# Heads of the last batch loaded early, row table and tile levels early, and 52 unread products in TensorE's waits, in an attention and mixture-of-experts block on one core

## The reference

```
x = x + attention(layernorm(x))                 # heads -> ctx @ W_O
xf = layernorm(x).reshape(-1, D)
logits = xf @ Wr / temp
topw, topi = top_k(logits, 2); topw = softmax(topw)
for e in range(8):
    a, g = split(xf @ W1[e] + b1[e])
    y = a * silu(g) @ W2[e] + b2[e]
    out += y * (weight of e for the token, 0 if not chosen)
x = x + out
```

## Time and profile before

| | before |
|---|---|
| median of 3 runs | 1049.57 us (1048.76 to 1050.04) |
| profiled execution | 1049.65 us, span 1047.8 us |
| busy PE, DVE, ACT, POOL | 958.1, 782.6, 555.0, 508.1 us |
| clock granted to TensorE, mean | 0.94 of full speed |
| chain that ended last: PE, DVE, DMA, ACT | 78%, 8%, 5%, 3% |

### The profile page before, as it was taken

How to read it: one execution, slowest core, us unless ns; L and a number is a source line. 1 busy time by engine, 2 the same in 40 slices (tenths; PEclk the granted TensorE clock), 3 DMA queues, 4 the chain that set the end, 5 groups by cost and what they waited for, 6 DMA issues and landing times.

```text
span 1047.8 us, 21901 instructions
## 1 busy us (share of the span) xinstructions
PE 958.1 (91%) x5804; PEld 574.1 (55%) x5805; DVE 782.6 (75%) x2291; ACT 555.0 (53%) x1202; POOL 508.1 (48%) x972
## 2 busy tenths in 40 slices
PE   4999899999999999999989956299999999999993
PEld 2444243333333333333345546288888888888883
DVE  3675999999999999999966556466766666676762
ACT  1555067777777777777763535143433334434431
POOL 5555536666666666666633745543322323233232
PEclk9999589999999999999997966599999999999998
DMA  3688966485867867644456588753555375333332
GB/s 98 215 266 213 234 137 153 93 257 99 257 153 216 250 156 209 150 90 89 89 149 184 188 217 275 224 161 52 140 134 131 50 210 136 55 50 56 54 51 35
DMA packets 107729, 156.53 MB, mean 149 GB/s; under 512 B 26944, under 2 KB 82240, under 8 KB 105088
## 3 DMA queue, kind: packets, MB, share of 16 engines
q1 hardware_dynamic: 83696, 128.03, 45.8%
q0 software_dynamic: 13296, 17.77, 9.8%
q10 hardware_dynamic: 10656, 9.78, 3.5%
HBM read 90.46 MB, written 64.69 MB: 148 GB/s over the span
## 4 chain that ended last, share of the span: by engine, by line
PE 78%; DVE 8%; DMA 5%; ACT 3%; issue 2%; POOL 1%; ACTq 1%; SPq 0%; DVEq 0%; POOLq 0%
PE bank L860 13%; PE bank L881 13%; PE bank L842 13%; PE bank L2020 6%; PE bank L2022 6%; PE bank L2021 6%; PE bank L2050 3%; PE bank L2052 3%; PE bank L2051 3%; PE bank L2034 3%; PE bank L1632 2%; DMA e_rows<-slot_rows 2%; DVE a_xn L314 2%; PE a_ckv L363 2%; PE bank L1996 1%
## 5 line engine op out<-in xcount | busy, mean ns | idle before, releaser
L816 ACT ACTIVATE b_prob<-bank 128x512 f32<-128x512 f32 (+3 forms) x768 | 311.9, 507 | 79.7 <-PE bank L860 78.9
L842 PE MATMUL bank<-b_k_st,b_q_st 96*128 96x512 bf16 (+3 forms) x768 | 255.6, 346 | 5.8 <-DVE b_neg_max L770 1.7
L770 DVE CUSTOM_DVE_ANT_0 bank<-bank,b_mask_max 128x256 f32<-128x256 f32 (+3 forms) x512 | 241.6, 510 | 22.2 <-PE bank L842 22.0
L860 PE MATMUL bank<-b_q_st,b_k_st 99*128 99x512 bf16 (+3 forms) x768 | 242.9, 334 | 4.0 <-ACT b_prob L816 2.0
L726 POOL TENSOR_SCALAR_AFFINE_SELECT b_prob<-b_prob 128x128 f32<-128x128 f32 x512 | 147.0, 300 | 188.5 <-ACT b_prob L816 184.2
L1846 POOL DMA_INDIRECT out_dram<-e_y,e_token x71 | 110.5, 1557 | 238.6 <-issue 158.0
L773 DVE TENSOR_REDUCE b_neg_max<-bank 128x1 f32<-128x512 f32 x256 | 175.8, 687 | 13.4 <-PE bank L842 11.2
L881 PE MATMUL bank<-b_prob,b_v_aug 128*32 128x512 f32 (+3 forms) x1536 | 146.3, 500 | 0.0
L842 PEld LDWEIGHTS bank<-b_k_st,b_q_st 96*128 96x128 bf16 x768 | 75.9, 99 | 109.3 <-DVE b_neg_max L770 52.1
L860 PEld LDWEIGHTS bank<-b_q_st,b_k_st 99*128 99x128 bf16 x768 | 74.8, 99 | 106.3 <-ACT b_prob L816 79.1
L2020 PE MATMUL bank<-w_ring,e_rowsT_hi 128*128 x284 | 125.3, 441 | 3.5 <-DVE e_rowsT_lo L1871 2.2
(11 more groups left out here) (203 smaller groups left out, 1470.7 us busy)
## 6 DMA issues: line engine op xcount, KB each, us to landing
w_parts<-w_ring SPq DMA_DIRECT2D x10, 1536.0 KB, 7.3
w_ring<-w_parts SPq DMA_DIRECT2D x10, 1024.0 KB, 7.6
e_rows<-slot_rows ACTq DMA_DIRECT2D x74, 129.0 KB, 2.1
w_raw<-in_L_ffn_W SPq DMA_DIRECT2D x8, 1024.0 KB, 5.2
ctx_cols<-b_ctx_out SPq DMA_DIRECT2D x16, 512.0 KB
q_parts<-a_part_q SPq DMA_DIRECT2D x8, 768.0 KB, 4.0
k_parts<-a_part_k SPq DMA_DIRECT2D x8, 768.0 KB, 4.8
b_q_st<-q_parts SPq DMA_DIRECT2D x16, 384.0 KB, 5.0
```

The source lines that it names most:

```text
L770: nc.vector.tensor_tensor_reduce(scores, scores, mask_max[:, HALF - width:HALF], -1.0, -MASKED, ALU.add, ALU.min, to).then_inc(max_done, 1)
L816: nc.scalar.activation(prob[n % NP][:, 0:width], prob_ps[n % NS][:, 0:width], ACT.Exp, scale=SCALE).then_inc(prob_ok, 1)
L842: nc.tensor.matmul(out[:, 0:width], q_st[g % RING][0:STACK, h, i * P:(i + 1) * P], k_st[g % RING][0:STACK, h, half * HALF:half * HALF + wi ...
L860: nc.tensor.matmul(prob_ps[n % NS][:, 0:width], k_st[g % RING][0:MAXROWS, h, j * P:(j + 1) * P], q_st[g % RING][0:MAXROWS, h, q0:q0 + widt ...
```

## The change

- The heads of batch 3 go to a buffer of their own, `last_heads`, in the last stage of the weight ring (the rows below and the order show it as `w_raw`), whose weights are loaded only in the expert stage. So `load_heads(3)` no longer waits for `project(2)`, and SP issues it right behind `load_den(3)`, ahead of `store_inverse(3)`.
- SP waits for `c_scale` of batch 3 to land before it stores x2 of batch 2 and what follows.
- DVE does `scale_heads(3)` ahead of `slots(1)`.
- DVE works out `m_tile_row` first among the tables; `level_ok` and `tile_row_ok` are signals of their own. ACT reads the first three levels as soon as they are there, starts its loads at `tile_row_ok`, and splits the first tile's rows between its second and third load. PE transposes the first tile's rows before it waits for the tables.
- PE does 12 products of 128x512 ahead of `counts(1)` and 40 behind `counts(3)`, into the bank `wide[-1]`, from weights that lie in `w_ring`.

```diff
+        self.last_heads = weights.raw[:, W_STAGES, 0, 0:DC * SEQ].rearrange("p (c n) -> p c n", c=DC)
...
+        self.jumped = self.fresh[:].bitcast(F32)
...
+    def heads_of(self, b):
+        return self.heads[:] if b < BATCH - 1 else self.last_heads
+
     def load_heads(self, sp, b):
-        if b:
+        if 0 < b < BATCH - 1:
             sp.wait_ge(self.proj_ok, b * PAIRS)
...
         self.load_den(sp, 3)
+        self.load_heads(sp, 3)
         self.store_inverse(sp, 3)
         self.load_scale(sp, 3)
-        self.load_heads(sp, 3)
         self.load_x(sp, 3)
+        sp.wait_ge(self.scale_in_ok, 16 * DC * BATCH)
         self.store_x2(sp, 2)
...
             then(nc.vector.tensor_reduce(tile_f[:], passed[:], AX.X, ALU.add))
+            then(nc.vector.tensor_tensor(passed[:], passed[:],
+                                         self.jump[:].unsqueeze(1).to_broadcast([P, TABLE, SEGMENTS]),
+                                         ALU.mult))
+            then(nc.vector.tensor_reduce(self.jumped, passed[0:1], AX.X, ALU.add))
+            then(nc.vector.tensor_tensor(same[:], self.row_of_tile[:], self.jumped, ALU.add))
+            then(nc.vector.tensor_scalar(self.tile_row[:], same[:], float(EXPERTS * REGION), None, ALU.min))
+            dve.sem_inc(self.tile_row_ok, 1)
...
         choose(1)
+        scale_heads(3)
         slots(1)
         filled_by_two()
-        scale_heads(3)
         shift(2)
...
+    def spare_products(self, pe, batches, count):
+
+        pe.wait_ge(self.x2_ok, batches * PAIRS)
+        for n in range(count):
+            self.nc.tensor.matmul(self.wide[-1][:], self.weights.ring[:, 0, 0, 0:P], self.weights.ring[:, 0, 0, 0:CHUNK],
+                                  start=True, stop=True)
...
+        self.spare_products(pe, 3, 12)
         self.counts(pe, 1)
...
         self.counts(pe, 3)
+        self.spare_products(pe, 4, 40)
...
-        act.wait_ge(route.tables_ok, 1)
+        act.wait_ge(route.level_ok, 1)
+        levels = [level_of(n) for n in range(AHEAD)]
         route.rows_written(act, BATCH - 2)
         route.tokens_written(act)
+        act.wait_ge(route.tile_row_ok, 1)
         for n in range(AHEAD):
-            load(n, n)
-        rows_high(0, 0)
+            load(n, n, levels[n])
+            if n == 1:
+                rows_high(0, 0)
...
+        rows_turned(0, 0)
         pe.wait_ge(route.tables_ok, 1)
-        rows_turned(0, 0)
         steps(pe, step)
```

More of the change, by code:

```diff
@@ L1077, in __init__ @@
         self.tables_ok = sem("r_tables_ok")
+        self.tile_row_ok = sem("r_tile_row_ok")
+        self.level_ok = sem("r_level_ok")
     def follow(self, turn_bank, prob_sc_ok, prob_ok, pv_ok, max_done, rows_ok, v_aug_ok, acc_out, ctx_st):
@@ L1311, in scale_heads @@
         def scale_heads(b):
+            heads = self.heads_of(b)
             dve.wait_ge(self.heads_in_ok, 16 * (b + 1))
@@ L1316, in scale_heads @@
                 half = slice(k // DC * CHUNK, (k // DC + 1) * CHUNK)
-                nc.vector.tensor_tensor(self.heads[:, k % DC, half], self.heads[:, k % DC, half],
+                nc.vector.tensor_tensor(heads[:, k % DC, half], heads[:, k % DC, half],
                                         self.scale[:, k % DC, half], ALU.mult).then_inc(self.heads_ok, 1)
@@ L1462, in full_tiles @@
             nc.vector.scalar_tensor_tensor(out=self.tile_level[:], in0=self.tile_index[0:1, :],
-                                           scalar=self.full_two[0:1, 0:1], in1=level[:], op0=ALU.is_ge, op1=ALU.add)
+                                           scalar=self.full_two[0:1, 0:1], in1=level[:], op0=ALU.is_ge,
+                                           op1=ALU.add).then_inc(self.level_ok, 1)
         def pad_slots():
@@ L1501, in tables @@
             then(nc.vector.tensor_scalar(same[:, 1:TABLE], same[:, 1:TABLE], 1.0, None, ALU.mult))
-            then(nc.vector.tensor_scalar(self.fresh[:], same[:], -16.0, 16.0, ALU.mult, ALU.add))
-            then(nc.vector.tensor_tensor(passed[:], passed[:],
-                                         self.jump[:].unsqueeze(1).to_broadcast([P, TABLE, SEGMENTS]),
-                                         ALU.mult))
-            then(nc.vector.tensor_reduce(tile_f[:], passed[:], AX.X, ALU.add))
-            then(nc.vector.tensor_tensor(same[:], self.row_of_tile[:], tile_f[0:1, :], ALU.add))
-            nc.vector.tensor_scalar(self.tile_row[:], same[:], float(EXPERTS * REGION), None,
-                                    ALU.min).then_inc(self.tables_ok, 1)
+            nc.vector.tensor_scalar(self.fresh[:], same[:], -16.0, 16.0, ALU.mult, ALU.add).then_inc(self.tables_ok, 1)
             dve.wait_ge(self.tables_ok, 1)
@@ L1930, in _, with level_of, load @@
     def _(act):
-        def load(n, c):
+        def level_of(n):
+            return act.value_load(entry(route.tile_level, n), min_val=1, max_val=3)
+        def load(n, c, level=None):
             act.wait_ge(y_ok, n + 1)
-            level = act.value_load(entry(route.tile_level, n), min_val=1, max_val=3)
-            act.wait_ge(landed, level)
+            act.wait_ge(landed, level_of(n) if level is None else level)
             act.sem_inc(load_turn, 1)
```

4 lines of the change are left out of this document (2 added, 2 removed).

## The result

The changed kernel is slower: 1053.51 us (median of 6; 1052.86 to 1055.58) against 1049.43 (median of 6), ratio 1.0045 with a 95% interval of 1.0031 to 1.0058. The forecast was 1044.3.

What follows compares the result with a forecast made beforehand. It took the kernel as bound by the chain up to the first expert product, with a fixed distance behind it. Normalise(3) earlier -1.7, tables -3.6 and products 0 made -5.3 on 1049.65: 1044.3 us, own range 1042 to 1046.5.

Steps and rivals of the forecast that it cites:

- I take 603.0, just behind the heads: SP's queue, batch 3: the inverse store lands and c_scale is issued at 603.0, bounds 601.97 and 603.6.
- I take 11.9 ... L = 614.9.: Batch 3's c_scale load takes 11.9 us and lands at L = 614.9, bounds 612.5 and 616.6.
- L + 18.8: POOL's scatter branch: batch 1's rows land and free first_row[1] for normalise(3) 18.8 us after c_scale lands, at 633.7.
- L + 17.4: Projection branch: project(3) lets normalise(3) start 17.4 us after c_scale lands, at 632.3, earlier than the scatter branch.
- Slower: Rival: the c_scale wait before slots(1) costs more than the tables give, c_scale landing past 620.2; 1052.4 us; chance 0.04.
- 14.6 us: From batch 3's normalisation to its logits on DVE, the work stays the same 14.6 us.
- Row table and levels early: -3.6.: Tables, ACT's first loads and PE's transposes bring the first expert product 3.6 us earlier, bounds -2.7 and -3.9.
- a first expert product later than 670: Sign that the prediction is wrong: the first expert product comes later than 670 in the new trace.
- The 12 products: 0: PE ahead of counts(1): 12 products delay counts(1) to 612.2 without cost or gain, 0.
- The 40 products ... 0: PE behind counts(3): the clock is lost again before the first expert product, so 0, with -2.6 as other end.
- a kept clock: Rival: the products hold the clock and the expert stage starts warm, 2.6 us more gained, 1041.7 us; chance 0.2.
- The end of the kernel lies a fixed distance behind the first expert product.: Expert stage: PE is busy 337.62 of 350 us, so only moving the first expert product's start, or the clock, counts.

Runs made afterwards that it cites:

- b_heads_behind: The changed kernel, with batch 3's heads in their own buffer but issued behind the c_scale loads; 1052.83 us, 1.0031 to the kernel before.
- a_dve_old: The changed kernel, with DVE doing slots(1) ahead of scale_heads(3) again; 1050.95 us, 1.0015 to the kernel before.
- y_after_no_y: The changed kernel, its first three loads of rows skipping y_ok and the first rows' splitting waiting for the last table; 1053.46 us, 1.0035 to before.
- c_no_products: The changed kernel without its 12 and 40 unread products; 1052.8 us, 1.0030 to the kernel before.
- m_46_products: l_all_early with 46 unread products behind the last counts; 1048.01 us, 0.9979 to the kernel before.
- d_tables_only: The kernel before with only the early row table, levels, loads and transposes; 1050.41 us, 1.0006 to the kernel before.
- n_weights_behind: l_all_early with expert 3's weights issued behind the last rows' landing; 1043.22 us, 0.9954 to the kernel before.
- u_split_weights: n_weights_behind with the last third of expert 3's weights issued eight tiles later; 1043.32 us, 0.9948 to the kernel before.
- j_act_early: d_tables_only with ACT's copy of batch 3's rows behind the third load and Silu's table loaded in ACT's idle stretch; 1052.67 us, 1.0027 to before.
- l_all_early: j_act_early with the first three loads of rows not waiting for y_ok; 1047.28 us, 0.9981 to the kernel before.
- o_46_weights_behind: m_46_products with expert 3's weights issued behind the last rows' landing; 1048.72 us, 0.9986 to the kernel before.
- p_before_weights_behind: The kernel before with only expert 3's weights issued behind the last rows' landing; 1053.02 us, 1.0033 to the kernel before.
- q_after_weights_behind: The changed kernel with only expert 3's weights moved behind the last rows' landing; 1056.46 us, 1.0071 to the kernel before.

## Why the prediction was wrong

*"I take 603.0, just behind the heads"*, for the inverses' landing. The order was right; `b_heads_behind`, without the heads ahead, has `c_scale` issued 2.2 us behind the store. The size was not: the heads took 8.2 us and not 6.3, and the inverses landed at 605.1. That is 606.6 in the frame of before, 3.6 later than forecast and outside the bound of 603.6. The prediction said that no row of before shows a small store behind a large load. The trace has one: SP issued batch 1's heads at 544.43, and they took 13.5 us; batch 2's inverses, issued behind them at 547.98, took 10.2 us and landed at 558.2, just behind the heads. I had not looked there.

*"I take 11.9 ... L = 614.9."* With the inverses this is the failing step that costs most. Counted as in the prediction, from the inverses' landing, `c_scale` took 13.0 us and not 11.9: it did not get faster without the heads beside it. In the seven kernels whose scaling waited for it, the scaling began 12.7 to 13.7 us behind its issue. So the scaling came at 618.22, which is 619.7 in before's frame, past the bound of 616.6; of the 4.8 us that L was too early, 3.6 are the inverses' and 1.2 `c_scale`'s. Underneath lies a wrong picture: that the wait was the heads' and would shrink if they came early. The heads early on SP's queue (25.1 to 27.0 us behind the ctx_cols store, in five kernels), late from their own buffer (25.9), early on another queue (25.9 and 25.3) or as before (24.5 to 26.9, in ten kernels) all end in the same place. Between the end of attention and the scaling about two megabytes and a chain of three small transfers share the same engines, and what goes first was paid by what came next.

*"L + 18.8"* and *"L + 17.4"*. Both branches were right in form: the scatter gated the normalisation at L + 19.5, and `a_dve_old` showed the other at L + 17.3. With L too early by 4.8, the rival *Slower* was what happened up to here. It was worked out as a scale load of 17 us; nearly the same lateness came in two pieces, 4.8 us of extra inverse store and 13.0 of load. I gave it 0.04 because I put the price on one transfer and not on the chain. Normalise(3) was to come 1.7 us earlier and came 3.8 later (46.45 against 42.66): 5.5 us of the miss. With DVE's old order, in `a_dve_old`, it came at 43.16: 2.1 us of that difference are the order's, 1.2 come from a scaling that was earlier in that trace.

*"14.6 us"* from the normalisation to the logits held: 14.63.

*"Row table and levels early: -3.6."* From the logits to the first expert product it was 23.90 and became 22.42, so -1.5. The missed part is the wait for `y_ok` in `load`. I had costed what DVE's table and ACT's reads do, and not gone through every wait of the function that issues. `y_after_no_y` gives 20.26, which is -3.6: the sum was right, the gate on it was not seen. That is 2.1 us of the miss. The sign set for this, a first expert product later than 670, came true (674.74).

*"The 12 products: 0"* and *"The 40 products ... 0"* held in the time (`c_no_products`), and the clock was lost at the place named. The Trainium skill (TensorE: Matmul & The Clock Gate, Part 1) wants idle gaps avoided. `m_46_products` left gaps of only 1.04 and 1.36 us ahead of the first expert product, and its clock stayed at 1.00 up to it, in agreement with that. The prediction priced a kept clock at 2.6 us; the median shows no gain, and the trace says why: the faster PE came sooner to rows that weren't there.

*"The end of the kernel lies a fixed distance behind the first expert product."* This unproved sentence cost 3.2 us, the last part of the miss. The distance was 373.9 before, 377.1 after, 380.5 in `y_after_no_y`, 379.3 in `d_tables_only` and 371.6 in `n_weights_behind` (373.2 in `u_split_weights`, whose profiled execution lies nearer to its median). PE is busy 96% from 690 on the earlier trace rows, but that window begins behind the first tiles. In these PE, at half clock, happened to hide ACT's copy and table load (3.2 us ahead of the first Silu) and a load of rows slowed by the weights. An earlier start or a faster one took that cover away, wait by wait: `e_hidden`, then the rows of the fourth or fifth tile, each with the clock behind it. `j_act_early`, `l_all_early` and `n_weights_behind` show this one after the other. In the changed kernel this accounts for 1.6 us of the 3.2, lost in the first two tiles. Another 1.4 come in one step some 83 us behind the first expert product, and this doesn't explain them.

Still open is that second step. The profiled executions of thirteen kernels, the changed one among them, lose 1.2 to 1.8 us between two tiles, 80 to 90 us behind the first expert product (the tiles are 4.87 us apart otherwise), where those of before, `j_act_early`, `l_all_early`, `n_weights_behind` and `u_split_weights` lose at most 0.4. In the changed kernel it is this pair of waits, while a later expert's weights are loading:

```profile
757.40 0.44 PE L2020 MATMUL bank<-m_ident,e_rows 128*128 128x128 f32 x2 [0.49 <-DMA e_rows<-slot_rows]
758.25 0.50 PE L2044 MATMUL bank<-w_ring,e_rowsT_hi 128*128 x1 [0.41 <-issue]
```

The load of these rows is issued 0.86 us behind the weights before and after; it took 5.7 us before and 7.7 after, and why I can't say. So 1.4 of the 5.5 us that the changed kernel lost behind the end of attention (2.3 and 3.2) have no cause shown. Open too is why the 46 products cost 3 us or more in `o_46_weights_behind`, beyond the wait shown (against `n_weights_behind` its trace loses 2.4 us in the first five tiles, and 2.7 in two steps 80 and 95 us behind the first expert product, the second of which every kernel here loses but `n_weights_behind`), and whether the two moves of ACT and the freed first loads are all needed for the gain of `n_weights_behind`.

## What to carry to other kernels

"Busy from here on" doesn't make the rest of the kernel a fixed length: look at the first tiles behind the start that you move, and ask of each of their waits how much slack (time to spare before it would hold the engine up) it has now and what hides it. Before you put a large load ahead of a chain of small ones, price the whole chain behind it, on whatever queue it is issued. Here the version that beats both kernels most clearly, `n_weights_behind`, kept the change's early row table and levels, took one gate off the first loads, cleared ACT ahead of its first Silu, and got a transfer that nobody needed yet out of the way; the last of these alone made the kernel slower.

## What the chip showed that I had not expected

- A megabyte under way delayed 64 KB on the same queue (6.39 us instead of 1.55) and on another one (6.01 and 5.4 us, where the sixteen other kernels have 2.3 to 3.5). The Trainium skill, DMA: Bandwidth & Descriptors, section Queues, rings and completion order, has an engine take one queue's descriptors in order; the second pair of numbers shows that this order isn't needed for a delay.
- Loads of 129 KB of rows that land in 2.0 to 4.2 us otherwise took 7.0 to 10.9 beside 3 MB of weights and the scatters (`j_act_early` to `m_46_products`), and 6.1 to 9.0 beside the weights alone (`n_weights_behind`, `p_before_weights_behind`, `q_after_weights_behind`).
- After the 40 products the clock stayed at 1.00 through the idle microseconds of 668 to 671 and was 0.72 in 671 to 673; with 46 products, which ended 1.0 us before the first rows, it never fell ahead of the first expert product.
